# Two layers of graph attention: making and writing the three parts of q in the dense phase, and loading x behind the edge lists

## The reference

```python
q = (x @ qw + qb).reshape(N, 8, 16)          # k, v the same way
alpha = jnp.sum(q[dst] * k[src], axis=-1) * SCALE
m = jax.ops.segment_max(alpha, dst, num_segments=N)
a = jnp.exp(alpha - m[dst])
a = a / jax.ops.segment_sum(a, dst, num_segments=N)[dst]
out = jax.ops.segment_sum(v[src] * a[:, :, None], dst, num_segments=N).reshape(N, 128)
return out + x @ sw + sb                     # layer 0, relu, layer 1
```

## Time and profile before

| | |
|---|---|
| time, median of 3 runs | 6403.74 us (6400.26 to 6405.14) |
| the profiled execution's own time | 6406.73 us |
| its span, first to last instruction | 6404.6 us |
| busy share PE, DVE, ACT, POOL | 53%, 64%, 24%, 65% |
| mean granted PE clock | 0.674 of full speed |
| dense phase of layer 0, of layer 1 | begins at 181.05, 1396.78 us |
| first gather of `conv_edges`, layer 0, layer 1 | 222.76, 1441.84 us |

### The profile page before, as it was taken

The page is one execution under the profiler, slowest core; times in us unless marked ns, Lnnn a source line. Parts: engine busy times, 40 slices in busy tenths (PEclk is TensorE's granted clock), DMA queues, the critical chain, the costliest instruction groups (busy, mean ns, idle before and its releaser), DMA issues. The chain is left out here.

```text
span 6404.6 us, 52242 instructions
## 1 busy us (share of the span) xinstructions
PE 3363.3 (53%) x13923; PEld 2068.4 (32%) x13923; DVE 4125.4 (64%) x5314; ACT 1519.8 (24%) x3187; POOL 4151.7 (65%) x4234
## 2 busy tenths in 40 slices
PE   3477776765677777673333334333334333333463
PEld 2455555554555555441111111111111111111221
DVE  5587777767777777765555554555554555555597
ACT  0022222211222222112222222222222222222221
POOL 0477777736777776337777776777776777777230
PEclk7577777776877777785555656655566565556686
DMA  0466666636666665563333332333332333333341
GB/s 22 139 202 197 199 197 193 198 97 189 194 197 197 193 198 170 201 191 105 105 105 105 105 103 83 105 105 105 105 105 89 102 105 105 105 105 105 138 154 61
DMA packets 541083, 877.89 MB, mean 137 GB/s; under 512 B 85205, under 2 KB 383297, under 8 KB 532622
## 3 DMA queue, kind: packets, MB, share of 16 engines
q0 software_dynamic: 167776, 479.21, 26.0%
q1 hardware_dynamic: 373032, 395.35, 19.2%
HBM read 553.75 MB, written 320.47 MB: 136 GB/s over the span
## 5 line engine op out<-in xcount | busy, mean ns | idle before, releaser
L1295 POOL DMA_INDIRECT big<-h_tab,big x2352 | 2219.4, 944 | 795.2 <-issue 795.2
L588 POOL DMA_INDIRECT big<-kv_tab,big x1664 | 1644.5, 988 | 699.7 <-issue 497.9
L1341 PE MATMUL psum<-big 128*128 128x512 f32 x1176 | 1086.6, 1079 | 1778.9 <-ACT big L1318 1778.6
L1378 DVE TENSOR_TENSOR psum<-psum,big 128x1024 f32<-128x1024 f32 x294 | 555.7, 1890 | 1337.6 <-DMA big<-h_tab,big 1337.6
L1341 PEld LDWEIGHTS psum<-big 128*128 128x128 f32 x1176 | 342.8, 322 | 2358.4 <-ACT big L1318 2055.1
L1312 ACT COPY big<-big 128x1024 f32<-128x1024 f32 x294 | 563.5, 1916 | 2097.1 <-DVE big L1361 2097.1
L772 PE MATMUL psum<-big 128*128 128x136 f32 x3328 | 706.0, 364 | 501.7 <-DVE big L830 312.3
L772 PEld LDWEIGHTS psum<-big 128*128 128x128 f32 x3328 | 606.3, 256 | 596.4 <-issue 570.6
L682 ACT COPY big<-psum 125x128 f32<-125x128 f32 x1408 | 376.5, 267 | 1510.0 <-PE psum L728 1438.0
L1361 DVE TENSOR_TENSOR_SCAN big<-big,psum 128x1024 f32<-128x1024 bf16 x294 | 669.0, 2276 | 0.1
L720 PE MATMUL psum<-big 128*128 x4992 | 581.9, 263 | 112.1 <-DVE big L801 111.8
(11 more groups left out here) (391 smaller groups left out, 3336.5 us busy)
## 6 DMA issues: line engine op xcount, KB each, us to landing
run_tab<-big SPq DMA_DIRECT2D x294, 512.0 KB, 2.7
snap_tab<-big SPq DMA_DIRECT2D x176, 448.0 KB
item_tab<-big SPq DMA_DIRECT2D x208, 272.0 KB
big<-loc_tab SPq DMA_DIRECT2D x104, 512.0 KB, 4.6
big<-h_tab,big POOLq DMA_INDIRECT x2352, 2.5
big<-kv_tab,big POOLq DMA_INDIRECT x1664, 3.4
snap_tab<-big SPq DMA_DIRECT2D x176, 52.0 KB
kv_tab<-big SPq DMA_DIRECT2D x12, 512.0 KB, 2.6
```

Of the source, the lines that this page charges most:

```text
L588: nc.gpsimd.indirect_dma_start(out=kv_ring[:, b % SLOTS, k, :], out_offset=None, in_=kv_tab, in_offset=bass.IndirectOffsetOnAxis(ap=src_it ...
L1295: nc.gpsimd.indirect_dma_start(out=got[j % RING][:, k * D:(k + 1) * D], out_offset=None, in_=h_tab, in_offset=bass.IndirectOffsetOnAxis(ap ...
L1341: ins_ = nc.tensor.matmul(bank[2 * (j % DEEP) + k][:, :], ea_T[j % DEEP], w_blocks[:, k * 512:(k + 1) * 512], start=True, stop=True)
L1378: nc.vector.tensor_tensor(by_feature(msg[j % DEEP]), by_feature(msg[j % DEEP]), got[j % RING].rearrange("p (t f) -> p f t", f=D), ALU.add) ...
```

## The change

It has two parts.

1. SP no longer loads `x` in the first block, but in the second, behind the loads of the edge lists, and waits for it there before it writes `loc_tab`. The first block keeps POOL's matrices and DVE's clearing of the padding.
2. q is made for four positions of 128 columns at a time ahead of skip. Its three parts are made in the dense phase, a quad at a time and with three quads under way at once (`thirds_of`): DVE evicts a quad, ACT rounds it, DVE subtracts, ACT rounds, DVE subtracts, ACT rounds. SP issues the two first loads of `loc_row`, then a write to `q_tab` a quad, waits for all of them, and issues the read to `q3`, in the same block. Skip's evictions follow those of q. The padding of `q3` is cleared by POOL, in layer 0 only. `conv_edges` has none of this left; PE waits there for `q_in` as before.

```diff
@@ first block
-                    nc.vector.memset(x[96:P, :], 0.0).then_inc(cleared, 1)
-                @block.sync
-                def _(sp):
-                    rows = a["x"].rearrange("(p t) d -> p (t d)", t=NT)
-                    sp.dma_start(x[0:96, :], rows[0:96, :]).then_inc(loads, 16)
-                    sp.wait_ge(cleared, 1)
-                    sp.dma_start(x[96:NODES_P, :], rows[96:NODES_P, :]).then_inc(loads, 16)
-                    sp.wait_ge(loads, 2 * 16)
+                    nc.vector.memset(x[96:P, :], 0.0)
@@ second block, sync, behind the edge lists
+                    rows_x = a["x"].rearrange("(p t) d -> p (t d)", t=NT)
+                    sp.dma_start(x[0:96, :], rows_x[0:96, :]).then_inc(x_in, 16)
+                    sp.dma_start(x[96:NODES_P, :], rows_x[96:NODES_P, :]).then_inc(x_in, 16)
                     sp.wait_ge(edges_in, 16 * (2 * (TB + 1) + TB))
+                    sp.wait_ge(x_in, 2 * 16)
@@ conv_edges, sync
-                        for i in range(NT // U):
-                            sp.wait_ge(split_done, i + 1)
-                            sp.dma_start(table(q_tab)[:, U * i:U * (i + 1), :], ...).then_inc(q_out[i % 2], 16)
-                        for h in range(2):
-                            sp.wait_ge(q_out[h], 16 * ((NT // U + 1 - h) // 2))
-                        sp.dma_start(q33[0:112, :, :], windows[0:112, :, :]).then_inc(q_in, 16)
-                        sp.dma_start(q33[112:WN, :, :], windows[112:WN, :, :]).then_inc(q_in, 16)
@@ conv_edges, vector
-                        nc.vector.memset(q3[P - 32:P, :], 0.0).then_inc(setup, 1)
-                        for i in range(NT // U):
-                            later(dve, q_out[i % 2], 16 * (i // 2))
-                            link_(nc.vector.tensor_copy(hi, q))
-                            link_(nc.vector.tensor_tensor(q, q, hi, ALU.subtract))
-                            link_(nc.vector.tensor_copy(mid, q))
-                            link_(nc.vector.tensor_tensor(q, q, mid, ALU.subtract))
-                            nc.vector.tensor_copy(lo, q).then_inc(split_done, 1)
@@ conv_linear, gpsimd
+                        if layer == 0:
+                            nc.gpsimd.memset(q3[P - 32:P, :], 0.0).then_inc(pads, 1)
@@ conv_linear, sync, behind the writes of kv_tab
+                        for k in range(2):
+                            sp.dma_start(loc_rows[k], loc_of(k)).then_inc(loc_in[k], 16)
+                        for g, (lo, hi) in enumerate(QUADS):
+                            sp.wait_ge(cast, casts_at(2, g))
+                            sp.dma_start(table(q_tab)[:, lo:hi, :], thirds_of[g % 3][...]).then_inc(q_out[g % 3], 16)
+                        for k in range(3):
+                            sp.wait_ge(q_out[k], 16 * ((last - 1 - k) // 3 + 1))
+                        if layer == 0:
+                            sp.wait_ge(pads, 1)
+                        sp.dma_start(q33[0:112, :, :], windows[0:112, :, :]).then_inc(q_in, 16)
+                        sp.dma_start(q33[112:WN, :, :], windows[112:WN, :, :]).then_inc(q_in, 16)
@@ conv_linear, scalar
+                        for n in range(last + 2):
+                            for k in range(3):
+                                g = n - k
+                                if 0 <= g < last:
+                                    lo, hi = QUADS[g]
+                                    if k == 0:
+                                        act.wait_ge(evac, many + g + 1)
+                                        later(act, q_out[g % 3], 16 * (g // 3))
+                                    else:
+                                        act.wait_ge(rest, rests_at(k, g))
+                                    nc.scalar.copy(thirds_of[g % 3][:, 0:hi - lo, k, :], q_n3[:, lo:hi, :]).then_inc(cast, 1)
@@ conv_linear, vector (PE: q's seven quads of 128 columns, then skip's seven)
+                        for n in range(last + 2):
+                            if n < last:
+                                four_out(many + n, n, q_n3, 2 * D)
+                            for k in (1, 2):
+                                g = n - k
+                                if 0 <= g < last:
+                                    lo, hi = QUADS[g]
+                                    dve.wait_ge(cast, casts_at(k - 1, g))
+                                    nc.vector.tensor_tensor(q_n3[:, lo:hi, :], q_n3[:, lo:hi, :], thirds_of[g % 3][:, 0:hi - lo, k - 1, :], ALU.subtract).then_inc(rest, 1)
+                        for g in range(last):
+                            four_out(many + last + g, g, skip3, 3 * D)
```

More of the change, by code:

```diff
@@ L187, in table @@
             return t.rearrange("(p t) c -> p t c", t=NT)
+        x_in, = dma_sems("x_in")
         with ExitStack() as ph:
-            cleared, loads, pool_step = fresh(ph, "cleared0", "loads0", "pool_step0")
+            pool_step, = fresh(ph, "pool_step0")
             with nc.Block() as block:
@@ L595, in build, with conv_edges @@
         row_d = small[:, 104:104 + P]
-        def conv_edges(layer, slot_in):
+        def conv_edges(layer, slot_in, loc_in, q_in):
             with ExitStack() as ph:
@@ L608, in conv_edges @@
                 here(4 * SLOTS * 2 * D)
-                loc_row = [here(4 * PAIR).bitcast(BF) for _ in range(2)]
+                here(8 * PAIR)
+                loc_row = loc_rows
                 hot_T = [here(4 * PAIR).bitcast(BF) for _ in range(2)]
@@ L644, in _ @@
                         nc.gpsimd.iota(node_row, pattern=[[1, NT], [NT, P]], base=0, channel_multiplier=0, allow_small_or_imprecise_dtypes=True).then_inc(setup, 1)
[L645 removed]
+                        pool.wait_ge(setup, 4)
                     @block.sync
                     def _(sp):
[L649 to L657 removed]
                         for t in range(-14, BATCHES + BEHIND + 3):
                             k = (t + 11) // 4
[L660 to L662 removed]
+                            if (t + 11) % 4 == 0 and 2 <= k < 2 * GI:
+                                sp.wait_ge(hotT_done, k - 1)
+                                sp.dma_start(loc_row[k % 2], loc_of(k)).then_inc(loc_in[k % 2], 16)
                             for n in counted_at(t - 2):
@@ L1025, in build, with conv_linear @@
         FIRST = 3
-        def conv_linear(layer, source, slot_in, scale_of=None, joined=None):
+        LQ = len(QUADS)
+        cast_order = [(k, n - k) for n in range(LQ + 2) for k in range(3) if 0 <= n - k < LQ]
+        rest_order = [(k, n - k) for n in range(LQ + 2) for k in (1, 2) if 0 <= n - k < LQ]
+        casts_at = lambda k, g: cast_order.index((k, g)) + 1
+        rests_at = lambda k, g: rest_order.index((k, g)) + 1
+        loc_rows = [area(B1 + 4 * SLOTS * 2 * D + 4 * PAIR * k, 4 * PAIR).bitcast(BF) for k in range(2)]
+        loc_of = lambda k: loc_tab[8 * k:8 * (k + 1), :].rearrange("(o i) e -> o (i e)", o=1).to_broadcast([P, 8 * PAIR])
+        def conv_linear(layer, source, slot_in, loc_in, q_in, scale_of=None, joined=None):
             groups = [[(lo, min(lo + 2, hi)) for lo in range(first_, hi, 2)] for first_, hi in QUADS]
@@ L1031, in conv_linear @@
             many = len(pairs)
-            outs_at = lambda q: q + 1 if q < many else many + 2 * (q - many + 1)
+            last = len(QUADS)
+            q_out = dma_sems("q_out0", "q_out1", "q_out2")
             with ExitStack() as ph:
+                pads, cast, rest = fresh(ph, "q_pads", "q_cast", "q_rest")
                 kv_in, qs_in, step, joined_done, tr_done, copied, mm_done, evac, tab_out = fresh(
@@ L1036, in conv_linear @@
                 turned = area(38600, NT * D)
+                thirds_of = [area(B1 + 19700 + 768 * k, 768).bitcast(BF).rearrange("p (t k d) -> p t k d", k=3, d=D) for k in range(3)]
                 with nc.Block() as block:
@@ L1087, in _ @@
                             pe.wait_ge(copied, g + 1)
-                            for _ in groups[g]:
-                                products(q, 0)
+                            for lo, hi in groups[g]:
+                                products(q, lo, hi, 0, 2 * D)
                                 q += 1
                         pe.wait_ge(qs_in, 16 * 4)
-                        for q in range(many, 2 * many):
-                            products(q, 2 * D)
+                        for at in (2 * D, 3 * D):
+                            for lo, hi in QUADS:
+                                products(q, lo, hi, at, D)
+                                q += 1
                     @block.vector
@@ L1514, in node_sums @@
             link(nc.vector.tensor_tensor(work3[:, lo:hi, :], agg[:, lo:hi, 0:D], skip3[:, lo:hi, :], ALU.add))
-        conv_in = dma_sems(*[f"conv0_slot{k}" for k in range(SLOTS)])
-        conv_linear(0, x, conv_in)
-        conv_edges(0, conv_in)
-        conv_finish(0)
-        conv_in = dma_sems(*[f"conv1_slot{k}" for k in range(SLOTS)])
-        conv_linear(1, work, conv_in, shares, node_sums)
-        conv_edges(1, conv_in)
```

(9 more changed lines are left out.)

33 lines of the change are left out of this document (13 added, 20 removed).

## The result

The changed kernel takes 6343.12 us (median of 4 runs, 6338.64 to 6348.53) against 6402.0 (6400.11 to 6405.14) for the kernel before in the same measurement: ratio 0.9913, 95% interval 0.99 to 0.9926, so 59 us less where 71 were forecast. The profiled execution has a span of 6346.8 us, 57.8 less than before. The table cuts the spans into stages. The marks are read from each kernel's timeline: DVE's first eviction of q (L1123 before, L1133 after), the first gather of `conv_edges`, the layer's last gather. "Rest" is `conv_finish`, the front of layer 1 and all that follows the convolutions.

The account below looks back on a forecast made before the run. The prediction took POOL's row of gathers, their late start and the stall behind slot 14 to bound each layer, plus the initial wait for x. Gains 17.5 + 26.2 + 26.9 = 70.6 us gave 6333, likeliest range 6319 to 6345 (0.68).

Parts of the forecast that it names:

- signs of being wrong: POOL still standing at the 15th batch, the gathers' mean moving from 0.985, or the first gather coming later than 215.
- the range's lower end: 6319 us: q's last part at 214.2 and no hold of SP, 4.4 + 9.5 us better over both layers.
- Part 1: Program start: x loaded behind the edge lists, so the second block starts at 4.92 in place of 22.45, 17.5 us gained.
- E: Rival, program start: moving x brings nothing because something else took the first 22 us too; time 6350, chance 0.04.
- The stall goes: Edge phase: POOL no longer waits behind slot 14, with 8 to 14 us in hand; gains 30.4 and 29.7 us.
- C: Rival, edge phase: the stall stays in part through PE's low clock and late q3; time 6349, chance 0.04.
- D: Rival, edge phase: each gather gets dearer beside DVE's work; slower than before above 0.043 us a gather, chance 0.03.
- the estimate of 5.3 us: Dense phase: 14 subtractions contending with 12 gathers at 0.44 us each, some 1.8 us a layer dearer; not in the sum.
- 7 evictions and 14 subtractions ... so DVE sets the pace: Dense phase, layer 0: DVE at 2.16 us a round against ACT's 1.8, so q's last part is ready at 216.4.
- The sum of that stage: First q eviction to first gather: first gather at 227.0 against 222.76, 4.2 us later in layer 0, 2.8 in layer 1.
- Rival A: Dense phase end: the block waits for the q3 reads to land, 7.5 to 13.5 us a layer; time 6348 to 6360, chance 0.10.
- Rival B: Dense phase: ACT's rounding and DVE's subtracting don't overlap, q_tab written 12 us later; time 6357, chance 0.07.

Follow-up runs that it names:

- x_only: The kernel before with only the x loads moved behind the edge lists: 6387.44 us, ratio 0.9976 to before.
- q_only: The changed kernel with the load of x back in the first block: 6366.77 us, ratio 0.9944 to before.
- buf7: The changed kernel with seven buffers for q's parts in place of three: 6337.09 us, ratio 0.9901 to before.
- first5: The changed kernel with FIRST = 5, 20 gathers in the dense phase in place of 12: 6343.12 us, ratio 0.9904 to before.
- after_again: The changed kernel itself measured once more, on a chip like the first: 6348.7 us, ratio 0.9913 to before.
- buf4: The changed kernel with four buffers for q's parts in place of three: 7421.26 us, ratio 0.9992, on the slower chip; again on one like the first 6336.28, 0.9897.
- loc_behind: The changed kernel with the two loc_row loads issued behind the writes to q_tab: 7436.13 us, ratio 1.001 to before, on the slower chip.
- best: The changed kernel with seven buffers for q's parts and the q3 reads issued at the edge phase's start: 6327.03 us, ratio 0.9881 to before.
- reads_later_again: The changed kernel with the q3 reads issued at the edge phase's start, on a chip like the first: 6337.41 us, ratio 0.99 to before.

## Why the prediction was right, and where it was off

The gain came from the two places that were forecast, and the time, 6343.12, lies in the likeliest range of 6319 to 6345. That it does is in part luck: of the 20 us that were too good in the forecast, 7.1 were given back by stages that it took as unchanged or valued lower (below); without them the time would have been 6350. One of the prediction's own signs of being wrong came: the first gather at 215.18, later than 215, although the dense phase had begun 2.7 us ahead of the forecast 163.5. The two other signs did not: POOL doesn't stand at the 15th batch, and the gathers' mean is 0.988 and 0.990 us where it was 0.985 and 0.991. And the range's lower end was mis-worked: with q's last part at 214.2 and SP not held, POOL's release at 221.42 would have ended the block, so at most some 4 us a layer could be gained and not 7, and the end is near 6325.

**Part 1** (-17.5): right. The block moved by 17.63, the stage by 20.5; in `x_only` by 20.4 with nothing else changed. The other 2.8 come in the block that follows. Timeline of its first two groups of matmuls, before and then in the changed kernel:

```profile
35.90 6.58 PE L284 MATMUL psum<-big,ones 128*128 128x512 f32 x8 [35.90 <-DVEq L347]
...
46.51 9.88 PE L291 MATMUL psum<-big 128*128 128x257 f32 x32 [3.22 <-DVEq L354]
```

```profile
18.45 5.12 PE L282 MATMUL psum<-big,ones 128*128 128x512 f32 x8 [18.45 <-DVEq L345]
...
27.59 8.89 PE L289 MATMUL psum<-big 128*128 128x257 f32 x32 [3.22 <-DVEq L352]
```

The same work takes 1.46 and 0.99 us less after PE stood idle for 18.45 us from the start of the program and not 35.90. Over the second group the windows show a mean granted clock of 0.81 in place of 0.72, that is more of it at 2.4 GHz and less at 1.2; over the first they show 1.00 in both. `q_only`, with the late start, has 6.76 and 9.97. It is not the idle time alone: `buf7`, with the early start, has 6.22 and 9.70, and takes 158.0 us from this block's start to the dense phase, where the other early kernels on chips like the first take 155.6 to 156.6 (late start: 158.7 and 159.4). The second group goes with its granted clock: 7.20 us at 1.00 in `first5`, 8.89 at 0.81, 9.70 at 0.74 in `buf7`, 9.88 at 0.72. What decides that clock, and what the first group's time, is left open. E (part 1 nothing) is refuted.

**The stall goes** (30.4 and 29.7): right in mechanism, 27.3 and 29.7 measured. The freed slot comes at 259.72 + 0.68 = 260.4, 36.1 behind PE's start (36.6 taken), and POOL asks at 215.18 + 56.7 = 271.9: 11.5 us in hand, within the 8 to 14. The timeline's line of that last use:

```profile
259.72 0.68 DVE L796 TENSOR_TENSOR big<-big 128x512 f32<-128x512 f32 x1
```

C is refuted. The 3 us missing in layer 0 are 820 gathers at 1.293 in place of 1.289 us; `after_again` has 1058.3.

**D, the dearer gathers:** refuted, 1.293 and 1.295 against 1.289 and 1.295. Four of the 12 gathers of the dense phase were lengthened (1.52, 1.35, 1.20 and 1.47 for 0.95), 1.7 us in all. The Trainium skill (GPSIMD Engine Reference, Key points) names the contention with VectorE instructions of two SBUF inputs, such as the new subtractions. The trace agrees that some gathers stretch beside them; the estimate of 5.3 us made from it was three times too high, and POOL was not the last engine, so nothing of it reached the time.

**The step that failed: "7 evictions and 14 subtractions ... so DVE sets the pace", last part of q ready at 216.4.** That is 15.0 us behind the first eviction, and it took 24.7 (205.60 - 180.89). The working counted DVE's and ACT's work and left out the third link: ACT may not overwrite a buffer before SP's write of it has landed. Three buffers and three quads under way leave no slack. The write is issued behind the third cast of a round and wanted landed before the first cast of the next: 1.66 + 2.5 = 4.2 us a round. The prediction held the number, 3.1 us to landing in the earlier trace rows, and used it only once, for the last write. The Trainium skill (DMA: Bandwidth & Descriptors, Anatomy of one DMA) gives, for transfers issued by GpSimd, a fixed cost of some 2 us that is mostly completion latency. These writes are issued by SP; taken over to them as an estimate, its fit makes 2.9 us of 384 KB, and the trace has a median of 2.5.

**The sum of that stage** in layer 0: forecast 227.0 - 201.35 = 25.65, measured 34.29. The casts +9.7, the last write's landing 2.56 for 3.5 (-0.9), SP's reads 4.95 for 5.7 (-0.75), and the way from SP's end to the first gather 2.07 for 1.4 (+0.7): +8.7. Layer 1 the same, 33.2 for 25.1. Over both layers this is 16.8 us. Of the rest the forecast was 3.1 too good for the gathers of layer 0, and 2.96, 2.2 and 1.9 too bad for the start, the front of layer 1 and the tail: -70.6 + 16.8 + 3.1 - 7.1 = -57.8, the change of the span.

**Rival A** (the block's end waits for `q3` to land): refuted as put. The block starts 0.6 us behind SP's end, and the two reads land (12.2 and 14.4 us after their issue) some 7 and 9 us later than that. Its doubt was well placed, though: POOL does hold a block's end for its own transfers, and `buf7` shows what that costs when the reads come early.

**Rival B** came nearer in the lateness of q's last part, 12 us where 9.7 were measured, but for another reason. ACT and DVE do overlap (six casts within 3.8 us at the start); what did not overlap is the landing of the writes. This reading rests on `buf7`, `buf4` and `loc_behind`: none, two and four waits with seven, four and three buffers, and the same four with the loads moved away.

Open: why `best`'s gathers run 2.6 to 3.4 us longer, with none of their instructions changed. The reads of `q3` beside them are not all of it: `reads_later_again` has them too and runs 0.5 and 1.5 us longer.

## What to carry to other kernels

Where a result is made in buffers and sent off by DMA, the round is the work or the landing of the transfer, whichever the number of buffers makes visible: count the buffers against the steps under way and put the landing time into the round. Before large transfers are issued at the end of a block, ask whether another engine's small transfer has still to land in it, for that landing can then take a multiple of its time (here 9.0 us, and POOL held 9.72 in place of 3.26). Issued one block later they cost neither that nor the issuing queue's time, as long as nothing at that block's start needs them (here the spare time of the 15th batch).

## What was not expected of the hardware

- POOL's end of a block waits for its gathers to land: 3.26 us from the last gather's end, 3.50 in `best`, 9.72 with 2.4 MB of reads issued 0.5 to 0.9 us ahead of it (`buf7`). Reads issued behind the last gather don't have this effect: the block then starts 0.6 us behind SP (`buf4`, and `first5` in layer 0).
- Two reads of `q_tab` into `q3`, 2100 and 281 KB, take 12.2 and 14.4 us to land in the changed kernel, a fifth to a quarter less than the 15.6 and 18.8 of the earlier trace rows; while they run the window of `buf7` has 228 GB/s at a DMA share over 1. Issuing the second holds SP 4.3 to 5.3 us in these kernels, 6.40 with the `loc_row` loads just ahead.
- PE's first matmuls of the program took 5.12 to 6.76 us for the same work in different kernels, for which the granted clock of the records gives no reason: it is 1.00 over them in each kernel that was measured (the one before, the changed one, `x_only`, `q_only`, `buf7`, `first5`, `buf4_again`, `best`).
- The kernel before took 6402 us on one chip and 7427 on another, at a mean granted clock of 0.673 to 0.678 in nine executions on a chip like the first and of 0.634 to 0.643 in 29 on the other. Beside that, the view of waits of `buf4` there puts 430.5 us of ACT's waiting in layer 0 down to "remote" and not to an engine of this core. What that is stays open.
